# One program for the delta rule and the gated output, in place of two in a row

## The reference, cut to what matters

```python
# L1_attn: delta rule with 4 heads of 64, in chunks
def step(S, inp):
    q_i, k_i, u_i, w_i = inp
    attn_i = jnp.where(lower_incl, q_i @ jnp.swapaxes(k_i, -1, -2), 0.0)
    u_adj = u_i - w_i @ S
    o_i = q_i @ S + attn_i @ u_adj
    S = S + jnp.swapaxes(k_i, -1, -2) @ u_adj
    return (S, o_i)
...
o = (1.0 - mix[..., None]) * o_d + mix[..., None] * ema_out
out = rms_norm(o, rms_w).reshape(b, l, H * dv) @ Wo
# L1_ffn: gates on every token, then one output projection
def step(c, xt):
    ft = jax.nn.sigmoid(xt @ wf.T + c @ uf.T + bf)
    it = jax.nn.sigmoid(xt @ wi.T + c @ ui.T + bi)
    gt = jnp.tanh(xt @ wc.T + c @ uc.T + bc)
    return (ft * c + it * gt, None)
h = jnp.tanh(jnp.einsum('tbi,oi->tbo', x, wo) + c_final @ uo.T + bo)
...
x = x + L1_attn(layernorm(x))
x = x + L1_ffn(layernorm(x))
```

## Time and profile before

| | us |
|---|---|
| median of 3 runs | 1435.75 (1435.06 to 1437.74) |
| profiled execution, device time | 1436.34 |
| its span, first to last instruction | 1434.6 |
| delta rule, first to last matmul block | 920.9 to 1252.5 |
| gated output, first matmul to the end | 1253.5 to 1434.6 |

### The profile page before, as it was taken

One profiled execution on the slowest core, in us unless ns is written; L12 is line 12 of the kernel. 1 busy time (PEld: TensorE's weight loads), 2 busy tenths in 40 slices (PEclk: granted clock), 3 DMA queues, 4 the chain that ended last, 5 costly groups with the idle time before them and its releaser, 6 DMA issues. The chain is left out here.

```text
span 1434.6 us, 36334 instructions
## 1 busy us (share of the span) xinstructions
PE 1277.0 (89%) x12853; PEld 951.4 (66%) x12854; DVE 820.7 (57%) x1882; ACT 463.3 (32%) x1085; POOL 496.5 (35%) x709
## 2 busy tenths in 40 slices
PE   7999999899999999838888887298999999889997
PEld 5888888767776777614554555287888888746565
DVE  6788889533222222248888877457566666435443
ACT  1211222132222222226767774011222222123332
POOL 4344666415411111065666432223343434210000
PEclk9999999889999999968888997558999999779999
DMA  9999910113311211122444434612643334000001
GB/s 309 349 370 340 328 49 31 38 48 109 113 59 60 64 59 59 48 73 95 138 122 119 114 107 136 129 50 74 117 115 89 94 94 147 2 0 30 29 22 37
DMA packets 219962, 156.60 MB, mean 109 GB/s; under 512 B 111744, under 2 KB 201344, under 8 KB 219840
## 3 DMA queue, kind: packets, MB, share of 16 engines
q1 hardware_dynamic: 204288, 129.11, 30.7%
q0 software_dynamic: 9312, 25.44, 5.4%
q10 hardware_dynamic: 6240, 0.39, 0.3%
HBM read 64.47 MB, written 90.44 MB: 108 GB/s over the span
## 5 line engine op out<-in xcount | busy, mean ns | idle before, releaser
L945 PE MATMUL ps_sc<-w,a_qeo 128*128 x568 | 183.1, 466 | 0.0
L753 DVE TENSOR_TENSOR a_stm<-a_vpad,ps_sc 128x352 f32<-128x352 f32 x71 | 37.0, 521 | 177.2 <-ACT a_vpad L517 177.2
L945 PEld LDWEIGHTS ps_sc<-w,a_qeo 128*128 128x128 f32 x568 | 104.0, 193 | 46.5 <-issue 2.5
L423 POOL DMA_DIRECT2D x_slots<-a_stm x66 | 36.4, 551 | 226.1 <-issue 226.1
L1585 PE MATMUL d_pp<-d_xT,d_w_p 128*128 128x512 f32 x192 | 112.1, 732 | 1.1 <-ACT d_xT L1320 1.1
L1477 DVE SCALAR_TENSOR_TENSOR d_cout<-d_cin,d_taps,d_cout 128x512 f32<-128x512 f32 x144 | 106.1, 747 | 6.1 <-ACT d_cout L1338 2.7
L915 PE MATMUL ps_kv<-w,a_stm 128*128 x426 | 105.7, 384 | 1.2 <-DVE a_stm L746 1.1
L915 PEld LDWEIGHTS ps_kv<-w,a_stm 128*128 128x128 f32 x426 | 79.2, 190 | 30.1 <-issue 12.5
L2328 PE MATMUL g_pp<-g_xT,g_w_g 128*128 128x512 f32 x192 | 90.8, 613 | 8.3 <-ACT g_xT L2219 8.3
L1253 POOL DMA_INDIRECT got<-x_slots,d_idx x64 | 75.5, 1180 | 18.7 <-issue 16.1
L517 ACT ACTIVATE a_vpad<-ps_sc 128x352 f32<-128x352 f32 x71 | 33.0, 464 | 140.0 <-PE ps_sc L945 140.0
(11 more groups left out here) (273 smaller groups left out, 2834.4 us busy)
## 6 DMA issues: line engine op xcount, KB each, us to landing
x_slots<-a_zeros SPq DMA_DIRECT2D x32, 1024.0 KB, 11.0
rec<-d_kve SPq DMA_DIRECT2D x32, 384.0 KB, 2.9
u_kve<-rec SPq DMA_DIRECT2D x32, 384.0 KB, 3.9
a_qeo<-x_slots SPq DMA_DIRECT2D x71, 128.0 KB, 2.0
x_slots<-a_stm POOLq DMA_DIRECT2D x66, 128.0 KB, 2.1
rec<-d_act_out SPq DMA_DIRECT2D x32, 256.0 KB, 3.7
u_qkT<-rec SPq DMA_DIRECT2D x32, 256.0 KB, 3.5
w<-in_w SPq DMA_DIRECT2D x4, 1408.0 KB, 14.0
```

Source lines behind the costliest of these rows:

```text
L753: dve.tensor_tensor(e_h[:, q, 0:HID], e_gate[:, q, :], ps_3[q], ALU.mult).then_inc(h_out, 1)
L945: mm = pe.matmul(ps, e_xT[:, q, k, :], w13[:, s, k, bass.ds(e_hidden, 1), :], start=(k == 0), stop=(k == KD - 1))
```

## The change

delta_rule and gated_output become one program, rule_and_gates, of the same shape: step(i, k) with DEPTH = 11. Gates are now computed for pairs of tiles (256 columns) in one PSUM bank, b_p. The extra work of a step i:

- TensorE: in an even step the four transposes of xn (between p1 and rest) and the projection of gate 0 (behind p2); in an odd step gate 1 (between p1 and rest) and gate 2 (behind p2); in every step from i = 10 the output matmuls of tile i-10 (behind u). The transposes of o3 move to the end of the step and y moves to the next step, ahead of low.
- VectorE: bn_stats and bn_aggr of tile i-5; in even steps the keep, new and cT passes for a pair; z of tile i-10, in odd steps xn for a pair, the residual of tile i-11.
- ScalarE: the Tanh of the gates, the copy to xT, the last Tanh.
- GpSimd: rstd for a pair in odd steps.
- SP: the gate weights behind the loads of tile 4, and the store of tile i-11 at the end of each step.
- The bias matmuls run once, at the end of step 6.

"Compact state": S is now 64 columns per pair of heads (128x2x64) without the zeros. The state reads for k and q become eight matmuls on 64 rows with 64 columns into one pair of banks (b_eo), in one block at the start of the step; they wait for share of the tile before, where the reads for q waited for o2. The state product gives four 64x64 blocks, and VectorE adds them to the old S (in place of ScalarE's two copies). The Gram products are four matmuls of 256 columns in place of eight of 128.

The diff, cut to what decides the order and the shapes:

```diff
@@ delta_rule -> rule_and_gates: buffers
-        S = sb("S", [P, 2, 2, P])
+        S = sb("S", [P, 2, 2, DH])
+        xT = sb("xT", [P, 2, KD, PAIR * P])
+        gates = sb("gates", [P, 3, 2, PAIR * P])
+        cT = sb("cT", [P, 2, KD, PAIR * P])
-        b_g = ctx.enter_context(nc.psum_tensor("u_bank_g", [P, 2, 2, 2, P], F32))
-        b_1, b_2, b_ku, b_s, b_o, b_y = [psum(f"bank{n}") for n in range(2, 8)]
+        gram = ctx.enter_context(nc.psum_tensor("u_gram", [P, 2, 2, 2, P], F32))
+        b_eo = ctx.enter_context(nc.psum_tensor("u_bank_eo", [P, 2, 4, 2, DH], F32))
+        b_1, b_2, b_y = [psum(f"bank{n}") for n in range(4, 7)]
+        b_p = ctx.enter_context(nc.psum_tensor("u_bank_p", [P, 2, PAIR * P], F32))
-        DEPTH = 5
+        DEPTH = 11
@@ sync
+                if isinstance(t, int) and t == GATES_AT:
+                    load_gate_weights(sp, gate_kept, w, gates_loaded)
...
+                w_ = i - 11
+                if has(w_, NT):
+                    wait_apart(sp, loaded, res_done, w_ + 1)
+                    sp.dma_start(out[bass.ds(w_ * P, P), :], res[:, (k - 11) % 2, :]).then_inc(sent[(k - 11) % 2], 16)
@@ gpsimd
+                if k % 2 and has(m, NT):
...
+                    pool.tensor_scalar(shifted[:, :], mom[:, at:at + 2, 1], EPS, None, ALU.add).then_inc(shift_done, 2)
+                    wait_apart(pool, loaded, shift_done, m + 2)
+                    pool.tensor_tensor(rstd[:, :], shifted[:, :], half[:, 0:PAIR], ALU.pow).then_inc(rstd_done, 2)
@@ scalar (step starts with the gate of the step before)
+                if before:
...
+                    act.wait_ge(p_done, 2 * (i - 9) + 2)
+                    if even:
+                        gate(2)
+                    else:
+                        wait(act, c_done, i - 9)
+                        gate(0)
+                if D_:
+                    act.wait_ge(ot_done, d + 1)
...
+                if now:
+                    act.wait_ge(p_done, 2 * (i - 8) + 1)
+                    if even:
+                        wait(act, gy_done, i - 10)
+                        act.activation(xT[:, q], b_p[:, :, :], ACT.Copy).then_inc(p_out, 1)
+                    else:
+                        gate(1)
...
-                if B:
-                    act.wait_ge(s_done, b + 1)
...
-                        z = act.activation(S[rows, bq, :, rows], b_s[rows, 0:256].rearrange("p (n c) -> p n c", n=2)[:, :, rows],
...
+                if W:
+                    act.wait_ge(z_done, w_ + 1)
+                    wait(act, res_done, w_ - 1)
+                    act.activation(ht[:, wq, :], zt[:, wq, :], ACT.Tanh).then_inc(h_done, 1)
@@ vector, between X32 and u(high)
+                if gated:
+                    dve.wait_ge(p_out, 2 * (i - 8))
+                    for b_ in range(2):
+                        dve.tensor_scalar(gates[:, 0, b_, :], gates[:, 0, b_, :], c0h[:, b_:b_ + 1], c0h[:, b_:b_ + 1], ALU.mult,
+                                          ALU.add).then_inc(keep_done, 1)
+                    dve.scalar_tensor_tensor(out=gates[:, 1], in0=gates[:, 1], scalar=1.0, in1=gates[:, 2], op0=ALU.add,
+                                             op1=ALU.mult).then_inc(new_done, 2)
+                if D_:
+                    wait_apart(dve, loaded, y_out, d + 1)
+                    dve.bn_stats(stats[:, :], tile_of(x_res, d)).then_inc(stats_done, 1)
...
+                if gated:
...
+                    dve.scalar_tensor_tensor(out=cT[:, gq2], in0=gates[:, 1], scalar=0.5, in1=gates[:, 0], op0=ALU.mult,
+                                             op1=ALU.add).then_inc(c_done, 2)
@@ vector, behind stm
+                if B:
+                    dve.wait_ge(s_done, b + 1)
+                    wait(dve, s_out, b)
+                    dve.tensor_tensor(S[:, bq], S[:, 1 - bq], b_1[:, 384:512].rearrange("p (n c) -> p n c", n=2), ALU.add).then_inc(s_out, 1)
+                if W:
+                    dve.wait_ge(gy_done, w_ + 1)
+                    wait(dve, h_done, w_ - 1)
+                    dve.tensor_tensor(zt[:, wq, :], b_y[:, 0:D], b_z[:, :], ALU.add).then_inc(z_done, 1)
@@ tensor
                 if B:
                     wait(pe, s_out, b)
-                    wait(pe, less2_done, b)
-                    for n in range(2):
-                        mm = pe.matmul(b_ku[:, col(n, P)], qkT[:, bs, 2 + n, :], S[:, 1 - bq, n, :], start=(n == 0), stop=True,
-                                       skip_group_check=True)
+                    wait(pe, share_done, b)
+                    for z, what in enumerate((2, 0)):
+                        for n in range(2):
+                            for e in range(2):
+                                rows = slice(64 * e, 64 * e + 64)
+                                mm = pe.matmul(b_eo[:, e, z, n, :], qkT[rows, bs, what + n, :], S[rows, 1 - bq, n, :],
+                                               start=(z == 0 and n == 0), stop=(z == 0), skip_group_check=True)
                     mm.then_inc(ks_done, 1)
...
+                if D_:
+                    pe.wait_ge(ot_out, d + 1)
...
+                if now:
+                    wait(pe, p_out, 2 * (i - 8))
+                    if even:
...
+                                mm = pe.transpose(b_p[:, n, j * P:(j + 1) * P], xn[:, j, n * P:(n + 1) * P], ident[:, :])
...
+                    else:
+                        gate(1)
...
-                        for z, what in enumerate((2, 0)):
-                            for e in range(2):
-                                rows = slice(64 * e, 64 * e + 64)
-                                mm = pe.matmul(b_g[:, e, z, n, :], qkT[rows, gs, 2 + n, :], qkT[rows, gs, what + n, :],
-                                               start=True, stop=True)
+                        for e in range(2):
+                            rows = slice(64 * e, 64 * e + 64)
+                            mm = pe.matmul(gram[:, e, n].rearrange("p z t -> p (z t)"), qkT[rows, gs, 2 + n, :], qkT[rows, gs, n::2, :],
+                                           start=True, stop=True)
...
+                if W:
+                    pair, cols = ((k - 10) // 2) % 2, slice(k % 2 * P, (k % 2 + 1) * P)
+                    pe.wait_ge(c_done, w_ + 2 if k % 2 == 0 else w_ + 1)
+                    if D_:
+                        pe.wait_ge(y_out, d + 1)
...
+                    for kd in range(KD):
+                        pe.matmul(b_y[:, 0:D], xT[:, pair, kd, cols], w_z[:, kd, :], start=(kd == 0), stop=False)
+                    for kd in range(KD):
+                        mm = pe.matmul(b_y[:, 0:D], cT[:, pair, kd, cols], u_z[:, kd, :], start=False, stop=(kd == KD - 1))
+                    mm.then_inc(gy_done, 1)
...
+                        for e in range(2):
+                            h = col(2 * n + e, DH)
+                            mm = pe.matmul(b_1[64 * e:64 * e + 64, 384 + n * DH:384 + (n + 1) * DH], kve[:, bs, 0, h], u[:, h],
+                                           start=True, stop=True)
...
+                if now:
+                    pe.wait_ge(p_out, 2 * (i - 8) + 1)
+                    gate(0 if even else 2)
```

More of the change, by code:

```diff
@@ L1005 @@
 SUB = 16
+PAIR = 2
+GATES_AT = 4
+GATE_LOADS = 11
+BIAS_AT = 6
 REC = 5 * D
@@ L1863, in step, with gate @@
                 a = i - 2
-                b, bq = i - 3, (k - 3) % 2
                 c = i - 4
-                G, A, B, C = has(g, NT), has(a, NT), has(b, NT), has(c, NT)
+                d = i - 5
+                w_, wq = i - 10, k % 2
+                G, A, C, D_, W = has(g, NT), has(a, NT), has(c, NT), has(d, NT), has(w_, NT)
+                now, even, q = gate_at(i, k)
+                before, _, _ = gate_at(i - 1, (k - 1) % 4)
+                def gate(n):
+                    for b in range(2):
+                        z = act.activation(gates[:, n, b, :], b_p[:, b, :], ACT.Tanh, bias=bias[:, 2 * n + b:2 * n + b + 1],
+                                           scale=0.5 if n < 2 else 1.0)
+                    z.then_inc(p_out, 1)
+                if before:
+                    if isinstance(i, int) and i == 9:
+                        act.wait_ge(bias_set, 4)
+                    act.wait_ge(p_done, 2 * (i - 9) + 2)
[6 more added lines that the diff above has]
+                    act.wait_ge(ot_done, d + 1)
+                    wait(act, y_done, d)
+                    act.activation(oT[:, :, :], b_y[:, 256:512].rearrange("p (n t) -> p n t", n=2), ACT.Copy).then_inc(ot_out, 1)
                 if C:
@@ L2053, in step @@
                     for h in range(H):
-                        mm = pe.matmul(b_ku[high, col(h, DH)], GU[:, bs, h, :], u[low, col(h, DH)], start=False, stop=True,
+                        mm = pe.matmul(b_eo[high, h % 2, 0, h // 2, :], GU[:, bs, h, :], u[low, col(h, DH)], start=False, stop=True,
                                        skip_group_check=True)
```

365 lines of the change are left out of this document (121 added, 244 removed).

## The result

The changed kernel takes 1487.3 us (median of 4 runs, 1479.1 to 1494.7) against 1436.7 for the kernel before on the same chip: 1.0347 times as long (95% interval 1.0300 to 1.0395). The forecast was 1422.5 us, 0.9% faster. The profiled execution has a span of 1477.5 us.

What follows compares the result with a forecast made beforehand. TensorE, busy nearly all the time, was taken as the bound, so only its waits and slow-clock time could go. 1025.1 + 344.6 + 47.6 + 4.1 = 1421.4 us of span, plus 1.1, gave 1422.5; range 1406 to 1441.

Steps and rivals of the forecast that it cites:

- Blocks of a step: TensorE's matmul blocks in a full step, i = 10 to 34: 13.07 us, plus 0.3 for changes of tiling.
- changes of tiling: Three more switches of matmul tiling per full step, at some 0.10 us each: 0.3 us added.
- New waits: TensorE waits in even steps, 0.6 us before u and 0.5 before the output, none in odd: mean 0.55 a step.
- Rival 1: Clock falls in even steps behind the new waits, about 2.9 us each; one per pair gives 1457 us; chance 0.14.
- Up to step 10: Stretch before the full steps: +7 us, 3 to 13, so step 10 begins at 1025.1 instead of 1018.1.
- Bias products fall into TensorE's wait and cost nothing: In step 6, bias matmuls are hidden by a TensorE wait; without it they would cost 2.7 us.
- The end: Steps 35 to 41: 42.6 us of matmuls and waits, +5 for the clock, then 4.1 for the last passes.
- rival 3: The drain after the full steps runs at half clock: about +20 us instead of +5, 1438 us; chance 0.08.
- Rival 2: Larger in-order waits, reads and tiling changes in full steps: 14.5 us a step, 1437 us, no change; chance 0.14.
- The clock column: TensorE's granted clock reads 1.00 from 1010 to 1370 us and some 0.8 to 0.9 behind.

Runs made afterwards that it cites:

- e8_straight_line: Changed kernel with VectorE's gate work moved so TensorE does not wait for it, and steps 16 to 31 written out instead of looped: 1432.5 us.
- the filler: Four extra 128x256 matmuls on useless data behind a1 in steps 3 to 9, first added to the changed kernel with VectorE's gate work moved: 1462.0 us.
- e6_both: Changed kernel with VectorE's gate work moved into gaps and, below step 10, the old places of o3's transposes and y: 1441.9 us.

## Why the prediction was wrong

The step that failed is the clock of TensorE: it was taken to rise in step 5 as before and to stand at 1.00 through the loop. Of the 56.1 us between forecast and profile, 20.0 lie before step 10, 18.6 are falls in the loop, 5.5 pauses at its turns, for which there was no term; only 11.5 come from the sizes of blocks and waits, and 0.5 from the end.

- **Blocks of a step: right.** Forecast 13.07 + 0.3 = 13.37 us without waits; measured 13.53 (27.05 a pair, e8_straight_line). Reads 1.04 (1.05), Gram 1.07 (0.95, at the worse bound), state product 0.38 (0.60). The 0.3 for changes of tiling was not measured apart.
- **New waits: right in place, short in size.** 0.6 + 0.5 in an even step were forecast; the brackets are 0.67 and 0.87, and an even step without a fall is 14.53 - 12.86 = 1.67 longer than one without the waits. What was mis-sized is the duration of cT by the nearest pass (0.69; it took 1.10) and of the two keeps (0.68; they took 1.03). With the blocks this is 344.2 - 332.7 = 11.5 us over the loop (344.2: next point).
- **Rival 1: the main thing missed in the loop.** It was worked out with its place, and given 0.14. A fall behind the waits costs 1.6 us, not 2.9, but eight of eleven pairs of waits had one, 12.6 us in all. Against it stood that waits of 0.24 had left the clock at 1.00, and that the added blocks are dense. Both were true and neither helped: the row that did apply, half clock behind 0.52, was in the prediction, with a wait as long as the ones forecast. Without falls and gaps the 24 steps would have taken 12 x 14.53 + 11 x 14.19 + 13.7 = 344.2 us, of 368.3; 5.5 of the rest are the gaps at the loop's turns, 18.6 the falls: 12.6 behind waits, 6.0 around gaps, most of it in step 20. The gaps had no row in the kernel before, whose loop shows one pause of 0.3 us (step 17) and none at its turns; the changed kernel's steps written out have none.
- **Up to step 10: the largest single error.** Forecast +7, came +27. That the clock would rise in step 5 was not put as a term; it was taken over from the kernel before. There it rose while 128-row reads of 128 columns were still in the step; with the compact state and nothing else of the change it stays down until step 11. "Bias products fall into TensorE's wait and cost nothing" failed: they took 5.1 us at half clock, in a step without a wait. That reads wait for share was right, but at half clock these waits were small (0.3 us, and 3.4 at step 8); they showed their size when the filler brought full clock back.
- **The end: right as a sum.** 63.6 forecast, 64.1 measured, at a clock of 0.92; rival 3 did not happen. That the sum is so close is in part luck: step 34 alone took 13.5 us, not 11.9, and the rest less than forecast.
- **Rival 2 was added up too low.** Its own terms give 13.07 + 0.25 + 0.6 + 0.9 = 14.8 us a step, not 14.5, and so some 1445 us instead of 1437, outside the range. It did not happen either way: steps without falls take 14.36 on average.
- **The clock column** was forecast at 1.00 from 1010 to 1370. It stood at 0.50 until 1024 and at 0.94 in the loop.

The Trainium skill (TensorE: Matmul & The Clock Gate, A second HAM failure mode) tells of short idle times between groups of matmuls, frequent ones, that make the clock go back and forth. The loop's trace agrees: two waits of 0.7 to 0.9 us behind each other, then half clock in eight of eleven cases. I had drawn on the section before it, on long gaps.

## What to carry to other kernels

Before work is merged into a loop at full clock, price each new wait of TensorE twice: the wait, and the half clock behind it; where a wait can be moved to a place with cover by reordering the other engine, do that before timing anything. When matmuls are made smaller (fewer rows, fewer columns), the same time per step at full clock does not mean the same clock: look at stretches at half clock without any idle time. And when the first of several causes is removed, look again, since here the waits, the loop's turns and the half clock of the first steps each hid part of the others: repairs of all three, filler included, turned 3.5% slower into 1.9% faster.

## What was not expected of the hardware

- TensorE at 1.2 GHz (granted clock 0.50) for 64.8 us with no idle time at all, in steps of small matmuls (e6_both, 950.7 to 1015.5); in the kernel before 15.5 us of it (944.7 to 960.2).
- Added work that makes a stretch shorter: 28 more 128x256 matmuls (56 instructions), 113.6 to 100.2 us, clock 0.56 to 0.83.
- A gap of 1.6 to 1.9 us on TensorE at each of three turns of a loop of four long steps (changed kernel). It is put down to no engine, and is neither there in the same steps as straight code nor at the turns of the loop before; the loop with the compact state alone and the old place of y has two at each turn, of 1.2 to 1.9 us. What makes the gap is open.
- A VectorE pass of 128x512 with two inputs took 0.68 us in one place (L2045) and 1.10 in another (L2067), in the same step; the slow one began while a GpSimd pass ran, and at a place where it began first it took 0.68.
